# The last stage's padded halves share an empty row, and only 65 of their 67 rows are copied

## The reference, cut to what matters

```python
x = x + _L0_conv_ref(_gn(x), ...)      # a recurrence over the 32 rows of the images
x = x + _L1_conv_ref(_gn(x), W, b, 4)  # the last stage

# _L1_conv_ref: x is (32, 128, 32, 32), W is (128, 128, 3, 3)
is3x3 = (i - n) % 4 == 0               # these pairs of channels have all nine taps
Wm = W * where(is3x3, full, center)    # the others have the centre tap alone
y = conv(x, Wm, padding=((1, 1), (1, 1))) + sum(b, axis=1)

# _gn: normalisation over 32 groups of 4 channels and all pixels of an image
```

## Time and profile before

| | us |
|---|---|
| median of 3 runs | 709.94 |
| lowest and highest | 704.29, 713.18 |
| the profiled execution | 712.78 |
| its span from the first to the last instruction | 711.0 |
| first copies of the last stage issued at | 490.46 |
| first tiled matmul at | 499.51 |

### The profile page before, as it was taken

One profiled execution on the slowest core, in us unless ns is written; L12 is line 12 of the kernel. 1 busy time (PEld: TensorE's weight loads), 2 busy tenths in 40 slices (PEclk: granted clock), 3 DMA queues, 4 the chain that ended last, 5 costly groups with the idle time before them and its releaser, 6 DMA issues.

```text
span 711.0 us, 15705 instructions
## 1 busy us (share of the span) xinstructions
PE 630.9 (89%) x5152; PEld 391.7 (55%) x5152; DVE 559.0 (79%) x1236; ACT 441.2 (62%) x779; POOL 426.0 (60%) x380
## 2 busy tenths in 40 slices
PE   1577889899999999999999999973899998988886
PEld 0233433378888888888888888851333333333332
DVE  5698998499999999999999999997576667666431
ACT  1595878777777777777777777774343444334310
POOL 0484687555555555555555555558676777577660
PEclk9998999999999999999999999995799999999997
DMA  9999900004441244442144443105799999999994
GB/s 224 238 265 274 151 5 8 1 0 60 59 60 31 28 59 59 59 59 37 22 59 59 59 59 44 15 1 129 192 283 254 284 267 251 262 254 269 274 258 126
DMA packets 96396, 90.61 MB, mean 127 GB/s; under 512 B 78240, under 2 KB 79520, under 8 KB 96288
## 3 DMA queue, kind: packets, MB, share of 16 engines
q1 hardware_dynamic: 89632, 71.09, 44.8%
q10 hardware_dynamic: 6720, 18.93, 10.0%
HBM read 35.07 MB, written 16.78 MB: 73 GB/s over the span
## 4 chain that ended last, share of the span: by engine, by line
PE 60%; SPq 21%; DVE 8%; DMA 3%; issue 3%; POOL 2%; ACT 2%; ACTq 0%; POOLq 0%; DVEq 0%
SPq L340 11%; PE ps L1009 7%; PE ps L1095 7%; SPq L346 6%; PE ps L1042 5%; PE ps L1046 4%; PE ps L1043 4%; PE ps L1056 4%; PE ps L1054 4%; PE ps L1055 4%; PE ps L1012 4%; PE ps L1000 4%; PE ps L959 3%; PE ps L960 2%; DMA shifted<-pad 2%
## 5 line engine op out<-in xcount | busy, mean ns | idle before, releaser
L731 POOL TENSOR_TENSOR fc<-gate,cell 128x352 f32<-128x352 f32 (+1 forms) x96 | 107.4, 1119 | 153.6 <-ACT gate L859 153.6
L766 POOL COPY shifted<-pad 32x1124 f32<-32x1124 f32 x128 | 142.9, 1116 | 58.6 <-DVE pad L646 52.4
L859 ACT ACTIVATE gate<-ps,gate_bias 128x352 f32<-128x352 f32 (+1 forms) x288 | 146.6, 548 | 47.6 <-PE ps L1046 31.8
L1095 PE MATMUL ps<-shifted,wt_hi 128*32 128x512 f16 x1536 | 110.7, 395 | 19.1 <-DMA shifted<-pad 19.1
L653 DVE SCALAR_TENSOR_TENSOR img<-ps,y_unscale,img 128x512 f32<-128x512 f32 x64 | 47.9, 748 | 82.9 <-PE ps L1095 82.8
L880 ACT ACTIVATE pad<-img,nbias,rstd 128x1024 f16<-128x1024 f32 x32 | 39.8, 1245 | 89.5 <-PE ps L1095 84.1
L739 POOL TENSOR_TENSOR img<-hT,xr 128x352 f32 (+3 forms) x96 | 87.0, 907 | 2.7 <-DVE hT L624 2.6
L408 DVE BATCH_NORM_STATS2 bn<-img 128x6 f32<-128x512 f32 x120 | 76.4, 680 | 10.7 <-DMA img<-in_x_dram 10.7
L721 POOL TENSOR_TENSOR lo<-xn,hi 128x1024 f16<-128x1024 f32 x32 | 68.1, 2131 | 19.0 <-PE ps L960 12.3
L1095 PEld LDWEIGHTS ps<-shifted,wt_hi 128*32 128x32 f16 x1536 | 35.5, 97 | 76.7 <-DMA shifted<-pad 24.0
L1042 PE MATMUL ps<-z_hi,wg_hi 128*128 128x352 f32 (+1 forms) x192 | 70.7, 371 | 2.3 <-ACT z_hi L848 2.2
(11 more groups left out here) (138 smaller groups left out, 1435.5 us busy)
## 6 DMA issues: line engine op xcount, KB each, us to landing
shifted<-pad SPq DMA_DIRECT2D x128, 140.4 KB, 4.3
shifted<-pad ACTq DMA_DIRECT2D x128, 140.4 KB, 4.3
img<-in_x_dram SPq DMA_DIRECT2D x128, 128.0 KB, 3.4
xr<-in_x_dram SPq DMA_DIRECT2D x64, 256.0 KB, 5.6
out_dram<-img SPq DMA_DIRECT2D x60, 256.0 KB, 4.7
shifted<-shifted SPq DMA_DIRECT2D x2, 562.0 KB, 6.1
out_dram<-img SPq DMA_DIRECT2D x16, 64.0 KB, 1.7
raw_c<-in_L_conv_W_dram SPq DMA_DIRECT2D x4, 144.0 KB, 3.2
```

The source lines that it names most:

```text
L731: pool.tensor_tensor(fc[s % 2][:, 0:n], gate[s % 2][0][:, 0:n], cell[:, W * b0:W * b1], ALU.mult).then_inc(fc_done, 1)
L766: pool.tensor_copy(flat(shifted[b % SLOTS][32:64, q]).bitcast(F32), flat(pad[b % SLOTS][32 * q:32 * q + 32]).bitcast(F32)).then_inc(unshif ...
L859: act.activation(gbank(s, m)[:, 0:n] if m == 1 else gate[p][m][:, 0:n], gbank(s, m)[:, 0:n], ACT.Tanh if gt == G_GATE else ACT.Sigmoid, bi ...
L1095: ins = pe.matmul(bank[32 * q:32 * q + 32], w[:, d, q, :], padded(shifted[b % SLOTS][:, q, part, :], s, d - 1, 0), start=False, stop=(m == ...
```

## The change: what it does

The two halves of `pad`, and of each block of `shifted`, now overlap by one row: the low half begins at `LOW_AT` = 33 rows of 33 = 1089 elements instead of 1124, so that the empty row below the high half is the one above the low half. A slot has `PADT` = 2214 elements per block instead of 2248. The copies (DMA and POOL) take the elements from `ROWS_AT` = 34 to `ROWS_END` = 2180, that is 2146 elements or 4292 bytes per partition, instead of 2246 (DMA) and 2248 (POOL). What lies before and behind that range in `shifted` is cleared once per slot by POOL, in six memsets at the start of the stage (`clear_edges`), behind which POOL waits before its first copy. The matmuls, the instructions of ScalarE and VectorE, and the number and order of all DMAs stay as they are; addresses in the two tensors change.

```diff
+LOW_AT = (H + 1) * PADW
+PADT = LOW_AT + PADN + 1
+ROWS_AT = 1 + PADW
+ROWS_END = ROWS_AT + (2 * H + 1) * PADW + 1
...
-            pad = [sb(f"pad{i}", [P, 2, PADN], F16, s2) for i in range(SLOTS)]
+            pad = [sb(f"pad{i}", [P, PADT], F16, s2) for i in range(SLOTS)]
-            shifted = [sb(f"shifted{i}", [P, Q, 2, PADN], F16, s2) for i in range(SLOTS)]
+            shifted = [sb(f"shifted{i}", [P, Q, PADT], F16, s2) for i in range(SLOTS)]
...
-        def padded(t, half, dh, dw):
-            at = 1 + (16 * half + 1 + dh) * PADW + dw
+        def padded(t, part, half, dh):
+            at = LOW_AT * part + 1 + (16 * half + 1 + dh) * PADW
             return t[:, at:at + 16 * PADW].rearrange("p (h w) -> p h w", w=PADW)[:, :, 0:W]
...
         def shift_to(slot, e, q):
-            return flat(shifted[slot][32 * e:32 * e + 32, q])[:, 1:2 * PADN - 1]
+            return shifted[slot][32 * e:32 * e + 32, q, ROWS_AT:ROWS_END]
         def shift_from(slot, e, q):
-            return flat(pad[slot][32 * q:32 * q + 32])[:, e:e + 2 * PADN - 2]
+            return pad[slot][32 * q:32 * q + 32, ROWS_AT + e - 1:ROWS_END + e - 1]
...
         def interior(t, part):
-            return t[:, part, 1 + PADW:1 + PADW + H * PADW].rearrange("p (h w) -> p h w", w=PADW)[:, :, 0:W]
+            at = LOW_AT * part + ROWS_AT
+            return t[:, at:at + H * PADW].rearrange("p (h w) -> p h w", w=PADW)[:, :, 0:W]
...
             def unshifted(b, q):
-                pool.tensor_copy(flat(shifted[b % SLOTS][32:64, q]).bitcast(F32),
-                                 flat(pad[b % SLOTS][32 * q:32 * q + 32]).bitcast(F32)).then_inc(unshifted_done, 1)
+                pool.tensor_copy(shifted[b % SLOTS][32:64, q, ROWS_AT:ROWS_END].bitcast(F32),
+                                 pad[b % SLOTS][32 * q:32 * q + 32, ROWS_AT:ROWS_END].bitcast(F32)).then_inc(unshifted_done, 1)
+
+            def clear_edges(slot):
+                for edge in (slice(0, ROWS_AT), slice(ROWS_END, PADT)):
+                    pool.memset(shifted[slot][0:96, :, edge].bitcast(F32), 0.0).then_inc(edges_zero, 1)
 
             pool.wait_ge(pads_zero, SLOTS)
+            for slot in range(SLOTS):
+                clear_edges(slot)
+            pool.wait_ge(edges_zero, 2 * SLOTS)
             for b in range(B):
                 pool.wait_ge(lo_done, b + 1)
```

More of the change, by code:

```diff
@@ L212, in build_network @@
         pads_zero = sem("pads_zero")
+        edges_zero = sem("edges_zero")
         bias_rows = sem("bias_rows")
@@ L367, in _ @@
             for slot in range(1, SLOTS):
-                sp.dma_start(shifted[slot][3 * 32:P].rearrange("p q a b -> p (q a b)"),
-                             shifted[0][3 * 32:P].rearrange("p q a b -> p (q a b)")).then_inc(ones_in, 16)
+                sp.dma_start(flat(shifted[slot][3 * 32:P]), flat(shifted[0][3 * 32:P])).then_inc(ones_in, 16)
             for b in range(B):
@@ L757, in _ @@
             pool.wait_ge(row_done, ROW_AHEAD + ITEMS)
-            pool.memset(flat(pad[0][:]).bitcast(F32), 0.0).then_inc(pads_zero, 1)
+            pool.memset(pad[0][:].bitcast(F32), 0.0).then_inc(pads_zero, 1)
             pool.wait_ge(pads_zero, 1)
-            pool.memset(shifted[0][3 * 32:P].rearrange("p q a b -> p (q a b)").bitcast(F32), ONES_PAIR).then_inc(ones_set, 1)
+            pool.memset(flat(shifted[0][3 * 32:P]).bitcast(F32), ONES_PAIR).then_inc(ones_set, 1)
             pool.wait_ge(ones_set, 1)
             for t in pad[1:]:
-                pool.memset(flat(t[:]).bitcast(F32), 0.0).then_inc(pads_zero, 1)
+                pool.memset(t[:].bitcast(F32), 0.0).then_inc(pads_zero, 1)
             def unshifted(b, q):
-                pool.tensor_copy(flat(shifted[b % SLOTS][32:64, q]).bitcast(F32),
-                                 flat(pad[b % SLOTS][32 * q:32 * q + 32]).bitcast(F32)).then_inc(unshifted_done, 1)
+                pool.tensor_copy(shifted[b % SLOTS][32:64, q, ROWS_AT:ROWS_END].bitcast(F32),
[3 more added lines that the diff above has]
+                    pool.memset(shifted[slot][0:96, :, edge].bitcast(F32), 0.0).then_inc(edges_zero, 1)
             pool.wait_ge(pads_zero, SLOTS)
+            for slot in range(SLOTS):
+                clear_edges(slot)
+            pool.wait_ge(edges_zero, 2 * SLOTS)
             for b in range(B):
@@ L1085, in dense_half @@
                     pe.matmul(y_bank(b, s).rearrange("p (h w) -> p h w", w=W), w[:],
-                              padded(pad[b % SLOTS][:, part, :], s, 0, 0), start=(m == 0), stop=False,
+                              padded(pad[b % SLOTS], part, s, 0), start=(m == 0), stop=False,
                               skip_group_check=True)
@@ L1095, in tiled_half @@
                             ins = pe.matmul(bank[32 * q:32 * q + 32], w[:, d, q, :],
-                                            padded(shifted[b % SLOTS][:, q, part, :], s, d - 1, 0), start=False,
+                                            padded(shifted[b % SLOTS][:, q], part, s, d - 1), start=False,
                                             stop=(m == 2 and d == 2), tile_position=(0, 32 * q), skip_group_check=True)
```

## The result

| | before | after |
|---|---|---|
| median, us (runs) | 709.61 (6) | 698.49 (6) |
| lowest and highest | 704.29, 713.30 | 697.44, 701.69 |
| profiled execution, its span | 712.78, 711.0 | 697.59, 695.8 |

The ratio is 0.9852 (95% interval 0.9812 to 0.9892), a gain of 10.5 us (7.7 to 13.3). It was forecast as 4.9 us with a range that ended at 699.5. Ratios leave out executions that took over 1.5% longer than the fastest of the same kernel.

A forecast was written before the change was run, and what follows sets the result against it. The prediction took the last stage's DMA copies as the bound: 4.65 us from shorter rows plus 0.25 us at the start, memsets and POOL 0, gave 4.9 us, so 709.94 - 4.9 = 705.0 us, range 699.5 to 711.

The forecast's parts named there:

- What bounds the kernel: Last stage: DMA copies set the pace at 6.41 us per image; TensorE next, 0.6 us per image below.
- The price of the shorter rows: DMA copies, last stage: 200 bytes less saves 11.5 ns per row, 0.184 us per image, 5.15 us over 28 images.
- The tenth taken off: Last stage: queue waits, engine idle time and the three-slot loop swallow a tenth, leaving 4.65 of 5.15 us.
- The tail: End of last stage: TensorE's 4.02 us wait for copies shrinks by under 0.4 us.
- The rival of the kept clock: End of last stage: a shorter last wait keeps TensorE at full clock, 2.5 us more gained, 702.5 us; chance 0.12.
- The start: Start of last stage: shorter copies of the first images bring the first tiled matmul 0.2 to 0.3 us sooner.
- Memsets and POOL: Start of last stage: six memsets take 0.9 us, hidden behind VectorE; POOL's copy falls to about 1066 ns; effect 0.
- Cost per copy instead of per byte: Rival, last stage's copies: issue and completion set the pace, so nothing is won, 709.9 us; chance 0.16.
- The estimate of 3.3 us: Alternative price from the Trainium skill's 435 GB/s: 7.4 ns per 200 bytes, 3.3 us over 28 images instead of 5.15.
- New addresses dearer: Rival, DMA copies: new start addresses and pitch make each row dearer, up to +7.4 us, 717.3 us; chance 0.07.
- The range: Median time of the changed kernel: 699.5 to 711 us, taking in the forecast and the rival without a gain.

The follow-up runs named there:

- e7: Changed kernel with DMA copies cut to the first 1074 elements of each row, leaving part of the result out; 693.79 us, ratio 0.9796.
- e13: Changed kernel with one of its eight DMA copies per image made by ScalarE itself; 692.84 us, ratio 0.9763.
- e14: Kernel before, rows of 4492 bytes kept, with one of eight DMA copies per image made by ScalarE; 694.38 us, ratio 0.9807.
- e11: Kernel before, unchanged, run again for a second trace; the traced execution took 704.87 us.
- e8: Changed kernel measured again, unedited, with more runs (the second measurement); 700.67 us, ratio 0.9895.
- e3: The shared empty row alone against the kernel before: 4424 bytes per DMA row from byte 2, no edge memsets; 705.00 us, ratio 0.9963.
- e2: Changed kernel with longer slots and DMA rows of 4492 bytes again, from the new start address; 708.56 us, ratio 1.0009.
- e5: Changed kernel with longer slots and DMA rows of 4892 bytes, the additional elements zeros; 722.66 us, ratio 1.0208.
- e12: Changed kernel with ScalarE's four copies in SyncE's order, run again for another trace; the traced execution took 714.04 us.
- e1: Changed kernel with pad and shifted moved one element on, start alignment as before, rows of 4294 bytes; 701.74 us, ratio 0.9921.
- m3: Only the last stage's DMA traffic, no compute: eight sections of 4292 or 4492 bytes from byte 68 or 2, order balanced; span 1020.7 us.
- e6: Changed kernel with ScalarE's queue issuing its four copies in order 0, 1, 2, 3 like SyncE's; 708.83 us, ratio 0.9991.

## Why the prediction was wrong, point by point

**What bounds the kernel: right.** The copies set the pace, TensorE was next at some 0.5 us per image. e7 (fewer bytes), e13 and e14 (fewer copies) all end at TensorE's pace, 11.7 to 11.9 us per pair, and with any of them TensorE's waits for copies are nearly gone (none in e7, 2.7 and 4.2 us in e13 and e14, half or more of it at the start).

**The price of the shorter rows: the mechanism right, the size wrong.** This is the step that failed: "I take 11.5 ns, between the two". One bound, 12.2 ns, was the mean price per byte of a row. The other, 10.8 ns, was the slope between rows of 256 and of 4096 bytes in the traffic of two other stages. Neither was taken from this stream at two sizes. Measured in the kernels, a pair of images went from 12.79 (the two traces of before) to 12.19 us (the two of after), 0.60 us or 19 ns for each of the 32 rows that an engine carries. The prediction had 0.37 per pair, of which it let 0.33 arrive. Over the twelve pairs of the earlier trace rows that is 7.2 us instead of 4.0, and this alone makes up the surplus of the second measurement.

Where the other 7 to 8 ns come from was not found. The traffic without its compute does not show them: its line over all lengths has 0.35 us per pair, and its 0.50 between the two lengths reaches down to 0.24. TensorE's clock does not either, since it was the full one in the long stretch of all four traces; here are e11 and e8:

```profile
530.00:680.00 150.00, 139.51 (x1870) 53.96 (x1873) 94.55 (x187) 58.59 (x53) 106.46 (x96) 1.00 0.94 265
...
530.00:680.00 150.00, 143.97 (x1939) 55.52 (x1931) 96.75 (x189) 58.73 (x53) 105.02 (x99) 1.00 0.92 269
```

A step between 4424 and 4492 bytes is not excluded: by the pairs, 0.45 of the 0.60 us lie there (e3), but e3's time gained only 2.6 us. So it stays open whether the surplus is a step in the rows' price or comes from the copies and the compute beside each other. The busy time of the DMA engines is no safe price either: e2 had 0.91 instead of 0.94 at equal bytes and the pair was no shorter.

**The tenth taken off: wrong.** The queue's own waits and the three-slot loop were to swallow some of the gain; the queue's waits for `lo` stayed (6.7 and 8.8 us before, 6.6 and 9.9 after), and the pair fell by more than the forecast price all the same. A loop can also work the other way: after a long wait TensorE can run a tiled half at a lower clock, and what follows comes later (e5, e12): 3.77 us behind the wait of 3.06 in e12, against 2.12 at full clock. The Trainium skill describes such a loop, in which each wait for a DMA lets the clock fall and the next tile pays for it ("TensorE: Matmul & The Clock Gate", section "HAM oscillation — how this bites in real kernels"). The traces agree for some of the waits and not for all: a half behind 3.11 us in e5 kept the full clock, the halves behind 2.34 to 3.06 us in e12 did not. So fewer long waits can return more than the bytes alone. In the twelve pairs of before and after the clock took no part; it bears on the tail, and on e2, e5 and e12.

**The tail: neither the forecast nor its rival as priced.** The rival of the kept clock had 0.12 and 2.5 us on top. In the traces before the tail was 21.95 and 16.75 us, after it 16.63 and 16.54: the long wait for image 30 belongs to some executions, and against it stood "the wait shrinks only by what the last two images' copies save". It shrank from 4.02 us to nothing between the first traces and was 1.20 in e11. It was no fixed part of the end that the change could shorten by 0.4, but a lag that comes and goes. In traces with rows of 4492 bytes a wait of 3.9 to 4.0 us stood there in two (before, e2) and not in e11; with 4424 bytes there was one of 3.6 us (e3), and with 4292 or 4294 none of over 2 us in the three with the copies in the order of the change (after, e8, e1). So shorter rows seem to make it rarer; the traces are few. This lag is why the first two traces are 15.2 us apart and the measurements 7.5 and 10.5.

**The start: small and about right.** The first tiled matmul comes 8.50 us after the first issue (8.62 in e8) instead of 9.05 (8.84 in e11); forecast 0.2 to 0.3 sooner.

**Memsets and POOL: right at 0.** 0.60 us for six (forecast 0.9) within VectorE's time. POOL's copy went to 1074 ns (forecast 1066).

**Cost per copy instead of per byte: refuted**, in e2 to e5, each with the same number of copies. With it falls the reading of the Trainium skill's fixed cost of about 2 us per DMA ("DMA: Bandwidth & Descriptors", section "Anatomy of one DMA — SWDGE (gpsimd) path", which gives it for DMAs issued by GpSimd) as a bound on the stage: 6.4 KB per copy were worth 7.5 us or more. The estimate of 3.3 us from the same page's 435 GB/s was too low by more than half, and the stream did not come near to that rate (263 to 270 GB/s before and after).

**New addresses dearer: refuted.** e2 has the new addresses and no loss, and in m3 the starts differ with both signs.

**The range: too narrow on this side.** It allowed some 3 us for the scatter of the runs and rows shorter by up to 14 ns. The bounds of the price were a mean and a slope from other traffic, and the 19 ns measured lie outside.

## What to carry to other kernels

Where DMA copies set the pace and the next engine is close behind, price a saving by what a whole period of the stream takes at two sizes, not by the mean time per byte; here the marginal price in the kernel was 1.5 times the mean one (19 against 12.2 ns), and the traffic alone did not show this. Take one traced execution's end as one draw: a second trace of the same kernel differed by 5.2 us in its last 20 us. Before trimming copies further, look for an idle engine that can take one: one of eight copies moved to ScalarE brought 14 to 17 us, on rows of either length, and it left little for the trimming to gain.

## What the runs showed of the hardware that had not been expected

- The order of four copies in one queue (e6) was worth 7 to 10 us at equal bytes, and executions of that kernel spread from 702.0 to 714.0 us.
- A saturated stream of equal DMAs with nothing beside it does not repeat: two sections of some 130 us with rows of 4892 bytes took 129.7 and 138.3 us.
- TensorE's clock after a wait: halves behind waits of 3.49, 3.53 and 3.81 us took 2.86, 3.05 and 3.77 instead of 2.12 us (e5), while the one behind a wait of 3.11 us in the same trace kept full clock. In e12 waits of 2.34 to 3.06 us were enough, and in e2 one of 2.02 us, behind which a half took 3.35 us.
